# GpSimd head by head, a ring of three for masked scores, and six value-output products made early in a fused attention and feed-forward kernel

## Chip, cores and metric

The kernel runs on one core of a Trainium2 chip. The metric is the device time of one execution in microseconds (us). Engines are called TensorE (PE), VectorE (DVE), ScalarE (ACT), GpSimd (POOL) and SyncE (SP), which issues the DMAs.

## What is computed

```python
# x is (2, 512, 512); 32 heads; ranks 192 (query) and 64 (key/value)
xn = layernorm(x)
q = rmsnorm(xn @ Wq_a, q_a_ln_w) @ Wq_b          # per head 128 + 64 (rotated)
ckv = xn @ Wkv_a
compressed, k_pe = ckv[..., :64], ckv[..., 64:]
kv = rmsnorm(compressed, kv_a_ln_w) @ Wkv_b      # per head 128 key + 128 value
scores = (q_nope . k_nope + rope(q_pe) . rope(k_pe)) * 192 ** -0.5
probs = softmax(where(causal, scores, min))
o = concat_heads(probs @ v) @ Wo
x = x + layernorm(o)
x = x + layernorm(ffn(layernorm(x)))             # silu(gate) * up, tiled weights plus rank-2 terms
```

## The kernel before

The work has four stages. The **first stage** (a loop over `t`, eight token blocks of 128) normalises x, turns it, multiplies by the low-rank weights and turns the results into `ql` and `kt`. The **attention** runs over 16 pairs of heads, `body(p)` on each engine. The **projection** multiplies by the products of value and output weights. The **feed-forward** part ends the kernel.

One pair is 16 units `k` (two batches, two heads, four query blocks of 128; block `i = k % 4` has `128 * (i + 1)` keys). The steps of a unit cross the engines: `scores` on PE (three matmuls into bank `k % 2`), `mask_and_max` on DVE (bank to `ss`), `exponent` on ACT (`ss` to `pr`), `turn_p` on PE, `move_p` on ACT, `output` on PE. At step k PE issues `scores` for unit k+2 ahead of `turn_p` for unit k, and DVE masks unit k+2. Every engine works its list strictly in the order written, and semaphores tie the lists together: `scores(n)` waits until the units up to n-2 are masked, since it writes over their bank.

Once a pair three other things are woven in:

- The weights of the next pair are formed: `absorb_query` on PE at k = 0, then `weights_hi` on ACT (four copies, at k = 1, lines 388 to 391), then `weights_lo` on DVE (four subtractions at k = 2, lines 652 and 653: two take one operand from a PSUM bank, the last two take both operands, `sq` and `w1_hi` or `w2`, from SBUF). Behind them in DVE's list stand `rotate_own` of the second head and the mask of unit 5.
- The rotated queries of both heads of a batch: `query` on PE, `rotate_swapped` and `rotate_own` on DVE, `add_rotated` on GpSimd (line 325), `query_hi` on ACT (line 397), `query_lo` on GpSimd (line 332, `qrot` minus `qt_hi`, both in SBUF). The result `qt_lo` is waited for by `scores` of that head.
- `absorb_output(p)` on PE at k = 8 (line 1087) multiplies a pair's value and output weights (`sv`, loaded by SP); ACT copies the bank to `vs` at k = 9 and SP stores it to DRAM, from where the projection reads it. It is needed by nothing in the attention.

In the last pair (15) there are no next weights. In pair 0 `weights_hi` stands at k = 3 and `weights_lo` at k = 4.

Of the kernel before, what the change touches and what calls it, by code (L numbers as in the profile page):

```python
# [40 lines left out]
XB = 5  # L41
# [3 lines left out]
UNITS = 2 * QB  # L45
PU = BATCH * UNITS
HID, RANK = 1376, 2
# [29 lines left out]
def build(nc, x_d, wa_d, lnw_d, cst_d, kcs_d, sq_d, sv_d, w13_d, bs_d, a13_d, a2_d, w2_d, b2_d, out_d):  # L77
# [34 lines left out]
    ss = att.take("ss", [P, 2, SEQ])  # L112
# [3 lines left out]
    att.at += 32 + 4 * QB * 2 * RKV  # L116
    pt = att.take("pt", [P, 2, 2, QB, SEQ])
    r8 = qswp[0:2 * QB, 0, 0:P]
    negmax = small[:, 0:8]
# [80 lines left out]
    def sems(phase, words):  # L200
# [5 lines left out]
        q_scaled q_doubled qn_made krot_parts kvn_made qk_turned qk_hi_made qk_split""")  # L206
    x_in = [nc.alloc_semaphore(f"x_in{t}") for t in range(TB)]
# [13 lines left out]
    with block:  # L221

        @block.sync
        def _(sp):
# [10 lines left out]
            sp.dma_start(sv[:, :], sv_d[0]).then_inc(a.sv_in, 16)  # L235
# [25 lines left out]
            load_sq(1)  # L261
            load_sq(2)
            send_r(0)
            load_sv(1)
            store_wvo(0)
            for p in range(1, PAIRS - 2):
                send_r(2 * p - 1)
                load_sq(p + 2)
                send_r(2 * p)
                load_sv(p + 1)  # L270
                store_wvo(p)
            send_r(2 * PAIRS - 5)
            send_r(2 * PAIRS - 4)
            load_sv(PAIRS - 1)
            store_wvo(PAIRS - 2)
# [3 lines left out]
            for k in range(PAIRS // 2):  # L279
                if k == 3:  # L280
                    send_r(2 * PAIRS - 2)
                if k == 4:
                    store_wvo(PAIRS - 1)
                if k >= 3:
                    sp.wait_ge(c.wv_split, 2 * (k - 2))
                if k == PAIRS // 2 - 1:
                    send_r(2 * PAIRS - 1)
                    sp.wait_ge(a.wvo_out, 16 * PAIRS)
                sp.dma_start(wv_raw[:, k % 3, :, :], wvo_d[2 * k:2 * k + 2].rearrange("a p n -> p a n"))\
                  .then_inc((c.wv_in0, c.wv_in1, c.wv_in2)[k % 3], 16)  # L290
# [20 lines left out]
        def _(pool):  # L311
# [23 lines left out]
            def body(p, last=False):  # L335
                for b in (1,) if last else (1, 0):
                    gi = 4 * p + (2 if b else 4)
                    pool.wait_ge(a.qt_split, gi)
                    for h in range(2):
                        add_rotated(gi + h, h)  # L340
                    for h in range(2):
                        query_lo(gi + h, b, h, gi + 2)
# [32 lines left out]
        def _(act):  # L375
# [23 lines left out]
            def exponent(U, k, s_first=False, old=None):  # L399

                n = P * (k % QB + 1)
                act.wait_ge(a.s_masked, U + 1)
                if not s_first:
                    act.wait_ge(a.p_turned, U - 3)
                if old is not None:
                    act.wait_ge(a.rinv_made, old)
                nc.scalar.activation(pr[:, k % 4, 0:n], ss[:, k % 2, 0:n], ACT.Exp, bias=negmax[:, k % 8:k % 8 + 1],  # L407
                                     scale=-1.0, accum_out=rsum[:, k:k + 1]).then_inc(a.exp_made, 1)
# [55 lines left out]
            def body(p, first=False, last=False):  # L464
                for k in range(PU):
# [18 lines left out]
                    if k in (2, 4):  # L484
                        h = (k - 2) // 2
                        query_hi(4 * p + 2 + h, 1, h, None if first else PU * (p - 1) + UNITS + QB * (h + 1))
                    if k in (10, 12) and not last:
                        h = (k - 10) // 2
                        query_hi(4 * p + 4 + h, 0, h, PU * p + QB * (h + 1))
                    if k == 9:  # L490
                        act.wait_ge(a.wvo_made, p + 1)
                        if not first:
                            act.wait_ge(a.wvo_out, 16 * p)
# [9 lines left out]
            for t in range(TB + 4):  # L503
                if 0 <= t - 3 < TB:
# [8 lines left out]
                      .then_inc(f.std_rms_made, 1)  # L513
                if 0 <= t - 1 < TB:
# [25 lines left out]
                if t == TB + 2:  # L540
                    exponent(0, 0, True)
# [102 lines left out]
        def _(dve):  # L644
# [26 lines left out]
            def mask_and_max(U, k, first=False):  # L671
# [3 lines left out]
                if not first:  # L675
                    dve.wait_ge(a.exp_made, U - 1)
                nc.vector.tensor_tensor_reduce(out=ss[:, k % 2, 0:n], in0=bank[k % 2][:, 0:n], in1=mask[:, SEQ - n:SEQ],  # L677
# [92 lines left out]
            for t in range(TB + 4):  # L770
# [44 lines left out]
                if t in (TB, TB + 1):  # L815
                    rotate_swapped(t - TB, t - TB, first=True)
                    rotate_own(t - TB, t - TB, first=True)
                if t in (TB + 2, TB + 3):
# [195 lines left out]
        def _(pe):  # L1014
# [68 lines left out]
            def absorb_output(p):  # L1083

                pe.wait_ge(a.sv_in, 16 * (p + 1))
                for h in range(2):
                    last = nc.tensor.matmul(bank[XB][RKV * h:RKV * (h + 1), :], sv[:, h * RKV:(h + 1) * RKV],  # L1087
                                            sv[:, 2 * RKV + h * D:2 * RKV + (h + 1) * D], start=True, stop=True)
# [16 lines left out]
            def body(p, first=False, last=False):  # L1105
                for k in range(PU):
# [5 lines left out]
                    if k == (2 if first else 0) and not last:  # L1112
                        if first:
                            pe.wait_ge(f.qk_split, TB - 1)
                        else:
                            pe.wait_ge(a.wvo_moved, p)
# [7 lines left out]
                    if k == 8:  # L1124
                        if last:
                            pe.wait_ge(a.wvo_moved, p)
                        else:
                            pe.wait_ge(a.wq_split, p + 2)
                        absorb_output(p)
# [18 lines left out]
            for t in range(TB + 4):  # L1148
# [20 lines left out]
                if t == TB:  # L1169
                    pe.wait_ge(f.qk_split, QB)  # L1170
                    for h in range(2):
# [12 lines left out]
                if t == 4:  # L1184
                    absorb_query(0)
                if t in (TB + 2, TB + 3):
# [184 lines left out]
```

## Time and profile before

| what | value |
|---|---|
| median of 3 runs | 632.92 us (631.91 to 633.07) |
| profiled execution | 632.73 us, its span 630.8 us |
| PE busy in the span | 590.5 us (94%) |
| DVE busy | 461.4 us (73%) |
| ACT busy | 400.0 us (63%) |
| GpSimd busy | 198.9 us (32%) |
| length of one pair in the steady part (233.00 to 258.33) | 25.33 us |

Times within the trace are from the span's start. "Idle" in brackets behind an instruction is how long its engine had stood still, and who let it go. An instruction's record on PE, ACT and DVE includes its pipeline, so that neighbouring records overlap a little.

### The profile page before, as it was taken

To read this page: it belongs to the slowest core of one execution; us is meant where nothing else is said; L and a number is where in the kernel's file an instruction comes from. 1 tells how busy PE (TensorE), PEld (TensorE's weight loads), DVE (VectorE), ACT (ScalarE), POOL (GpSimd) and SP (SyncE) were. 2 spreads that over 40 slices of the span, in tenths; PEclk is the share of its full clock that TensorE was granted. 3 is DMA by queue.
4 is the path that set the end of the run, shared out by engine and by line. 5 is a ranking of instruction groups with operands and counts; after the bars stand their busy time and mean duration, and the time that the engine had idled before them with its cause. 6 is when DMAs were issued, how large, how long until landed. Compare 5 with 4: busy or idle time off the path is not lost.

```text
span 630.8 us, 10967 instructions
## 1 busy us (share of the span) xinstructions
PE 590.5 (94%) x3336; PEld 427.7 (68%) x3336; DVE 461.4 (73%) x1235; ACT 400.0 (63%) x1157; POOL 198.9 (32%) x172
## 2 busy tenths in 40 slices
PE   4786999999999999999999999999989999978996
PEld 4675767677677676776776767767658888754564
DVE  5876677677776777777767777777867888878466
ACT  4454677777777677766776777668753545264343
POOL 3134333443344334433353444344000000024630
PEclk9898999999999999999999999999989999999998
DMA  8100212312132122221331213205465000001003
GB/s 316 31 1 16 87 47 89 95 54 71 56 104 78 48 84 76 78 72 52 97 89 48 82 55 101 71 19 153 154 209 226 2 0 2 0 30 50 1 14 121
DMA packets 19561, 46.93 MB, mean 74 GB/s; under 512 B 2608, under 2 KB 3120, under 8 KB 19248
## 3 DMA queue, kind: packets, MB, share of 16 engines
q1 hardware_dynamic: 19504, 46.23, 22.8%
q8 instruction: 28, 0.46, 0.3%
q14 instruction: 29, 0.24, 0.1%
HBM read 39.80 MB, written 6.42 MB: 73 GB/s over the span
## 4 chain that ended last, share of the span: by engine, by line
PE 50%; issue 15%; DVE 15%; POOL 9%; ACT 9%; DMA 1%; POOLq 0%; SPq 0%; DVEq 0%; ACTq 0%
PE bank L1017 11%; PE bank L1019 9%; PE bank L1018 9%; PE bank L1072 7%; PE bank L1060 6%; POOL qrot L325 6%; ACT pr L407 3%; POOL qt_lo L332 3%; PE bank L1087 3%; DVE qswp L664 2%; DVE qrot L669 1%; DVE ss L677 1%; ACT pt L415 1%; DVE dot L865 1%; ACT qt_hi L397 1%
## 5 line engine op out<-in xcount | busy, mean ns | idle before, releaser
L677 DVE CUSTOM_DVE_ANT_0 ss<-bank,cst 128x128 f32<-128x128 f32 (+3 forms) x256 | 124.2, 490 | 95.6 <-PE bank L1019 75.0
L415 ACT ACTIVATE pt<-bank 128x128 f32<-128x128 f32 (+3 forms) x256 | 110.3, 431 | 88.4 <-PE bank L1060 88.3
L325 POOL TENSOR_TENSOR qrot<-qrot,qswp 64x512 f32<-64x512 f32 x64 | 81.9, 1280 | 208.2 <-DVE qrot L669 208.1
L407 ACT ACTIVATE pr<-ss,small 128x128 f32<-128x128 f32 (+3 forms) x256 | 142.4, 556 | 4.2 <-DVE small L677 4.0
L1060 PE MATMUL bank<-ident,pr 128*128 128x128 f32 x640 | 117.1, 281 | 0.6 <-ACT pr L407 0.6
L1017 PE MATMUL bank<-kt_hi,qt_hi 128*128 128x128 f32 (+3 forms) x256 | 101.0, 395 | 7.9 <-DVE small L677 4.5
L1060 PEld LDWEIGHTS bank<-ident,pr 128*128 128x128 f32 x640 | 74.5, 141 | 49.5 <-ACT pr L407 28.8
L332 POOL TENSOR_TENSOR qt_lo<-qrot,qt_hi 128x512 fp32r<-128x512 f32 x64 | 82.0, 1290 | 29.2 <-ACT qt_hi L397 27.9
L1072 PE MATMUL bank<-pt,kvn 128*64 128x256 f32 (+3 forms) x512 | 86.2, 448 | 0.7 <-ACT pt L415 0.7
L1019 PE MATMUL bank<-kt_hi,qt_lo 128*128 128x128 f32 (+3 forms) x256 | 82.9, 324 | 0.0
L1018 PE MATMUL bank<-kt_lo,qt_hi 128*128 128x128 f32 (+3 forms) x256 | 82.7, 323 | 0.0
L1017 PEld LDWEIGHTS bank<-kt_hi,qt_hi 128*128 128x128 f32 x256 | 48.8, 190 | 17.0 <-DVE small L677 9.1
L1017 PE MATMUL bank<-wv,o_s 128*128 128x512 f32 x128 | 52.2, 408 | 2.4 <-DVE wv L703 2.4
L1018 PE MATMUL bank<-wv,o_s 128*128 128x512 f32 x128 | 51.1, 399 | 0.0
L1019 PE MATMUL bank<-wv,o_s 128*128 128x512 f32 x128 | 51.0, 398 | 0.0
L1019 PEld LDWEIGHTS bank<-kt_hi,qt_lo 128*128 128x128 f32 x256 | 48.6, 190 | 2.8
L407 ACT ACTIVATION_READ_ACCUMULATOR pr<-ss,small 128x1 f32 x256 | 49.8, 194 | 0.0
L1018 PEld LDWEIGHTS bank<-kt_lo,qt_hi 128*128 128x128 f32 x256 | 49.3, 193 | 0.1
L1072 PEld LDWEIGHTS bank<-pt,kvn 128*64 128x64 f32 x512 | 29.9, 135 | 27.7 <-ACT pt L415 11.9
L370 POOL TENSOR_TENSOR fs<-gu 128x512 f32<-128x512 f32 (+1 forms) x6 | 8.2, 1366 | 124.5 <-DVE gu L951 124.3
L663 DVE TENSOR_TENSOR qswp<-bank,cst 32x512 f32<-32x512 f32 x64 | 44.5, 695 | 2.0
L664 DVE TENSOR_TENSOR qswp<-bank,cst 32x512 f32<-32x512 f32 x64 | 44.2, 691 | 0.9
(163 smaller groups left out, 1072.5 us busy)
## 6 DMA issues: line engine op xcount, KB each, us to landing
sv<-sv SPq DMA_DIRECT2D x16, 576.0 KB, 5.0
rsb<-rinv_scratch SPq DMA_DIRECT2D x64, 128.0 KB, 2.9
sq<-sq SPq DMA_DIRECT2D x16, 448.0 KB, 3.3
wvo_scratch<-vs SPq DMA_DIRECT2D x16, 256.0 KB, 4.8
wv_raw<-wvo_scratch SPq DMA_DIRECT2D x8, 512.0 KB, 4.8
xa<-x SPq DMA_DIRECT2D x8, 256.0 KB, 5.0
x<-x SPq DMA_DIRECT2D x1, 2048.0 KB, 9.6
out<-yo SPq DMA_DIRECT2D x8, 256.0 KB, 2.0
```

The costliest lines, as they stand in the source:

```text
L325: nc.gpsimd.tensor_tensor(qrot[RKV:P, h, :], qrot[RKV:P, h, :], qswp[RKV:P, h, :], ALU.add)\
L332: nc.gpsimd.tensor_tensor(qt_lo[:, b, h, :], qrot[:, h, :], qt_hi[:, b, h, :].bitcast(F32), ALU.subtract)\
L407: nc.scalar.activation(pr[:, k % 4, 0:n], ss[:, k % 2, 0:n], ACT.Exp, bias=negmax[:, k % 8:k % 8 + 1], scale=-1.0, accum_out=rsum[:, k:k + ...
L415: nc.scalar.activation(pt[:, b, h, 0:i + 1, i * P:(i + 1) * P], bank[2 + k % 2][:, 0:(i + 1) * P].rearrange("p (j q) -> p j q", q=P), ACT. ...
L663: nc.vector.tensor_tensor(qswp[64:96, h, :], G[96:128, :], sin1[96:128, :], ALU.mult)
L664: nc.vector.tensor_tensor(qswp[96:128, h, :], G[64:96, :], sin1[64:96, :], ALU.mult)
L677: nc.vector.tensor_tensor_reduce(out=ss[:, k % 2, 0:n], in0=bank[k % 2][:, 0:n], in1=mask[:, SEQ - n:SEQ], scale=-SCALE, scalar=3.4e38, op ...
L1017: nc.tensor.matmul(out, w_hi, x_hi, start=start, stop=False)
L1018: nc.tensor.matmul(out, w_hi, x_lo, start=False, stop=False)
L1019: return nc.tensor.matmul(out, w_lo, x_hi, start=False, stop=stop)
L1060: last = nc.tensor.transpose(bank[2 + k % 2][:, j * P:(j + 1) * P], pr[:, k % 4, j * P:(j + 1) * P], ident[:, :])
L1072: last = nc.tensor.matmul(bank[4][RKV * h:RKV * (h + 1), j * P:SEQ], kvn[:, QB * b + j, 0:RKV], pt[:, b, h, j, j * P:SEQ], start=(j == 0), ...
```

## The change

Three edits, of which two move instructions.

1. GpSimd works head by head: per batch it now adds head 0, subtracts head 0, adds head 1, subtracts head 1, where it did both adds and then both subtractions. ACT issues `query_hi` of head 0 at k = 1 and 9 (pair 0: 2 and 9) and that of head 1 at 4 and 12; before it was 2, 4, 10 and 12.
2. `ss` has three buffers. The buffer of unit k is `RING[k]`; DVE waits for the exponent two units back only where the ring reuses a buffer after two units, which by `BACK` is at k = 1 and k = 15.
3. Products 0 to 5 of `absorb_output` are issued in the first stage behind iterations 4 to 7 (`EARLY`: number, bank, copies that must have been made), from six loads `sve` that stand behind x and the constants in SP's list, and are copied by ACT to `pr` and `ss` and stored. In the attention pair p makes product p + 6, so that pairs 10 to 15 make none. The first mask and the first exponent wait until the six stores have landed.

```diff
 UNITS = 2 * QB
+RING = (0, 1, 2, 0, 1, 2, 0, 1, 2, 0, 1, 2, 0, 1, 2, 1)
+BACK = [next(d for d in range(1, 17) if RING[k - d] == RING[k]) for k in range(16)]
 PU = BATCH * UNITS
+EARLY = {4: ((0, 7, 0),), 5: ((1, 7, 1),), 6: ((2, 7, 2), (3, 6, 0)), 7: ((4, 7, 3), (5, 6, 4))}
+NE = 6
...
     qswp = att.take("qswp", [P, 2, SEQ])
-    ss = att.take("ss", [P, 2, SEQ])
+    ss = att.take("ss", [P, 3, SEQ])
...
     vs = att.take("vs", [P, D])
-    att.at += 32 + 4 * QB * 2 * RKV
+    att.at += 32
...
     r8 = qswp[0:2 * QB, 0, 0:P]
+    sve = Map(nc, att.at - 4 * 4 * QB * SEQ, att.at).take("sve", [P, NE, SV_COLS])
+    early = [pr[:, j, :] for j in range(4)] + [ss[:, j, :] for j in range(NE - 4)]
...
         q_scaled q_doubled qn_made krot_parts kvn_made qk_turned qk_hi_made qk_split""")
+    sve_in = [nc.alloc_semaphore(f"sve_in{j}") for j in range(NE)]
...
             sp.dma_start(cst[:, :], cst_d).then_inc(f.cst_in, 16)
-            sp.dma_start(sv[:, :], sv_d[0]).then_inc(a.sv_in, 16)
+            for j in range(NE):
+                sp.dma_start(sve[:, j, :], sv_d[j]).then_inc(sve_in[j], 16)
+            sp.dma_start(sv[:, :], sv_d[NE]).then_inc(a.sv_in, 16)
...
-            load_sq(1)
-            load_sq(2)
-            send_r(0)
-            load_sv(1)
-            store_wvo(0)
-            for p in range(1, PAIRS - 2):
-                send_r(2 * p - 1)
-                load_sq(p + 2)
+            for j in range(NE):
+                if j == 2:
+                    load_sq(1)
+                sp.wait_ge(a.wvo_moved, j + 1)
+                sp.dma_start(wvo_d[j], early[j]).then_inc(a.wvo_out, 16)
+            for p in range(PAIRS - 1):
+                if p:
+                    send_r(2 * p - 1)
+                if p + 2 < PAIRS:
+                    load_sq(p + 2)
                 send_r(2 * p)
-                load_sv(p + 1)
-                store_wvo(p)
-            send_r(2 * PAIRS - 5)
-            send_r(2 * PAIRS - 4)
-            load_sv(PAIRS - 1)
-            store_wvo(PAIRS - 2)
+                if p + NE + 1 < PAIRS:
+                    load_sv(p + NE + 1)
+                if p + NE < PAIRS:
+                    store_wvo(p + NE)
...
                     send_r(2 * PAIRS - 2)
-                if k == 4:
-                    store_wvo(PAIRS - 1)
...
                 for b in (1,) if last else (1, 0):
-                    gi = 4 * p + (2 if b else 4)
-                    pool.wait_ge(a.qt_split, gi)
                     for h in range(2):
-                        add_rotated(gi + h, h)
-                    for h in range(2):
-                        query_lo(gi + h, b, h, gi + 2)
+                        gi = 4 * p + (2 if b else 4) + h
+                        pool.wait_ge(a.qt_split, gi)
+                        add_rotated(gi, h)
+                        query_lo(gi, b, h, gi + 1)
...
                     act.wait_ge(a.rinv_made, old)
-                nc.scalar.activation(pr[:, k % 4, 0:n], ss[:, k % 2, 0:n], ACT.Exp, bias=negmax[:, k % 8:k % 8 + 1],
+                nc.scalar.activation(pr[:, k % 4, 0:n], ss[:, RING[k], 0:n], ACT.Exp, bias=negmax[:, k % 8:k % 8 + 1],
...
                         weights_hi(p + 1)
-                    if k in (2, 4):
-                        h = (k - 2) // 2
+                    if k in ((2, 4) if first else (1, 4)):
+                        h = k // 4
                         query_hi(4 * p + 2 + h, 1, h, None if first else PU * (p - 1) + UNITS + QB * (h + 1))
-                    if k in (10, 12) and not last:
-                        h = (k - 10) // 2
+                    if k in (9, 12) and not last:
+                        h = k // 12
                         query_hi(4 * p + 4 + h, 0, h, PU * p + QB * (h + 1))
-                    if k == 9:
-                        act.wait_ge(a.wvo_made, p + 1)
-                        if not first:
-                            act.wait_ge(a.wvo_out, 16 * p)
+                    if k == 9 and p + NE < PAIRS:
+                        act.wait_ge(a.wvo_made, p + NE + 1)
+                        act.wait_ge(a.wvo_out, 16 * (p + NE))
...
                       .then_inc(f.std_rms_made, 1)
+                for j, b, _ in EARLY.get(t - 1, ()):
+                    act.wait_ge(a.wvo_made, j + 1)
+                    nc.scalar.activation(early[j], bank[b][:, :], ACT.Copy).then_inc(a.wvo_moved, 1)
...
                 if t == TB + 2:
+                    act.wait_ge(a.wvo_out, 16 * NE)
...
                 dve.wait_ge(a.s_made, U + 1)
-                if not first:
+                if BACK[k] == 2 and not first:
                     dve.wait_ge(a.exp_made, U - 1)
-                nc.vector.tensor_tensor_reduce(out=ss[:, k % 2, 0:n], in0=bank[k % 2][:, 0:n], in1=mask[:, SEQ - n:SEQ],
+                nc.vector.tensor_tensor_reduce(out=ss[:, RING[k], 0:n], in0=bank[k % 2][:, 0:n], in1=mask[:, SEQ - n:SEQ],
...
                     rotate_own(t - TB, t - TB, first=True)
+                if t == TB + 2:
+                    dve.wait_ge(a.wvo_out, 16 * NE)
...
-            def absorb_output(p):
...
-                pe.wait_ge(a.sv_in, 16 * (p + 1))
+            def absorb_output(j, b=XB, w=sv):
...
+                pe.wait_ge(a.sv_in if j >= NE else sve_in[j], 16 * (j - NE + 1) if j >= NE else 16)
                 for h in range(2):
-                    last = nc.tensor.matmul(bank[XB][RKV * h:RKV * (h + 1), :], sv[:, h * RKV:(h + 1) * RKV],
-                                            sv[:, 2 * RKV + h * D:2 * RKV + (h + 1) * D], start=True, stop=True)
+                    last = nc.tensor.matmul(bank[b][RKV * h:RKV * (h + 1), :], w[:, h * RKV:(h + 1) * RKV],
+                                            w[:, 2 * RKV + h * D:2 * RKV + (h + 1) * D], start=True, stop=True)
...
                         else:
-                            pe.wait_ge(a.wvo_moved, p)
+                            pe.wait_ge(a.wvo_moved, min(p + NE, PAIRS))
...
                         output(2 * p - 1, 1, [2, 3])
-                    if k == 8:
-                        if last:
-                            pe.wait_ge(a.wvo_moved, p)
-                        else:
-                            pe.wait_ge(a.wq_split, p + 2)
-                        absorb_output(p)
+                    if k == 8 and p + NE < PAIRS:
+                        pe.wait_ge(a.wq_split, p + 2)
+                        absorb_output(p + NE)
...
                     pe.wait_ge(f.qk_split, QB)
+                    pe.wait_ge(a.wvo_moved, NE)
...
                     absorb_query(0)
+                for j, b, moved in EARLY.get(t, ()):
+                    if j == 3:
+                        pe.wait_ge(a.wq_split, 1)
+                    if moved:
+                        pe.wait_ge(a.wvo_moved, moved)
+                    absorb_output(j, b, sve[:, j, :])
```

On GpSimd in any pair from 1 to 14 (`qrot` is the rotated query, `qt_lo` its low part), rows of the kernel before:

```order
L325 TENSOR_TENSOR qrot<-qrot,qswp 64x512 x2
L332 TENSOR_TENSOR qt_lo<-qrot,qt_hi 128x512 x2
L325 TENSOR_TENSOR qrot<-qrot,qswp 64x512 x2
L332 TENSOR_TENSOR qt_lo<-qrot,qt_hi 128x512 x2
L325 TENSOR_TENSOR qrot<-qrot,qswp 64x512 x2
```

and of the changed kernel:

```order
L332 TENSOR_TENSOR qrot<-qrot,qswp 64x512
L339 TENSOR_TENSOR qt_lo<-qrot,qt_hi 128x512
L332 TENSOR_TENSOR qrot<-qrot,qswp 64x512
L339 TENSOR_TENSOR qt_lo<-qrot,qt_hi 128x512
L332 TENSOR_TENSOR qrot<-qrot,qswp 64x512
```

The subtraction of the first head has moved ahead of the addition of the second.

On ACT in a pair from 1 to 14, steps k = 1 to 3 (`w_hi` and `w_58` are the next pair's weights), rows of the kernel before:

```order
L407 ACTIVATE pr,small<-ss,small 128x512
L388 ACTIVATE w_hi<-bank 128x2x64
L389 ACTIVATE w_hi<-sq 128x2x64
L390 ACTIVATE w_58<-bank 128x2x64
L391 ACTIVATE w_58<-sq 128x2x64
L415 ACTIVATE pt<-bank 128x3x128
L407 ACTIVATE pr,small<-ss,small 128x128
L397 ACTIVATE qt_hi<-qrot 128x512
```

and of the changed kernel:

```order
L413 ACTIVATE pr,small<-ss,small 128x512
L394 ACTIVATE w_hi<-bank 128x2x64
L395 ACTIVATE w_hi<-sq 128x2x64
L396 ACTIVATE w_58<-bank 128x2x64
L397 ACTIVATE w_58<-sq 128x2x64
L403 ACTIVATE qt_hi<-qrot 128x512
L421 ACTIVATE pt<-bank 128x3x128
```

The copy to `qt_hi` now follows straight behind the four weight copies, two instructions earlier.

On PE at the end of iteration 6 of the first stage (products with `wa`, then the turns of x), rows of the changed kernel, where before the turns of x followed the products at once:

```order
L1029 MATMUL bank<-wa_lo,xt_hi 128x320
L1030 MATMUL bank<-wa_hi,xt_lo 128x320
L1098 MATMUL bank<-sve 64x512 x4
L1163 MATMUL bank<-ident,xn 128x128 x4
L1174 MATMUL bank<-ident,qn 128x128
```

Two early products (four rows of 64x512) stand between them.

## Rows read from the trace of the kernel before

**Rows 1.** Stretches: length, PE, PEld, DVE, ACT, POOL busy, clock share, DMA

```profile
233.00:258.33 25.33, 25.00 (x155) 17.77 (x154) 18.36 (x52) 18.58 (x60) 10.24 (x9) 1.00 0.25 75
```

**Rows 2.** Waits, whole run: us in total, times, longest us

```profile
DVE ss L677 <- ACT pr L407: 19.5, 31, 0.7
...
PEld bank L1017 <- POOL qt_lo L332: 7.0, 15, 2.9
...
PE bank L1017 <- DVE small L677: 4.5, 15, 0.7
```

**Rows 3.** Timeline of PE, a steady pair

```profile
238.70 0.50 PE L1017 MATMUL bank<-kt_hi,qt_hi 128*128 128x512 f32 x1 [0.27 <-DVE small L677]
```

**Rows 4.** Timeline of DVE, the same pair

```profile
236.99 0.29 DVE L652 TENSOR_TENSOR w_lo<-sq,w_hi 128x128 fp32r<-128x128 f32 x1
237.29 0.29 DVE L653 TENSOR_TENSOR w<-sq,w 64x128 fp32r<-64x128 f32 x1
237.61 0.69 DVE L669 TENSOR_TENSOR qrot<-bank,cst 128x512 f32<-128x512 f32 x1
238.22 0.41 DVE L677 CUSTOM_DVE_ANT_0 ss<-bank,cst 128x256 f32<-128x256 f32 x1
...
252.61 0.69 DVE L677 CUSTOM_DVE_ANT_0 ss<-bank,cst 128x512 f32<-128x512 f32 x1 [0.60 <-ACT pr L407]
...
254.87 0.42 DVE L677 CUSTOM_DVE_ANT_0 ss<-bank,cst 128x256 f32<-128x256 f32 x1 [0.66 <-ACT pr L407]
```

**Rows 5.** Timeline of ACT, the same pair

```profile
236.02 0.32 ACT L391 ACTIVATE w<-sq 128x128 fp32r<-128x128 f32 x1
236.22 0.50 ACT L415 ACTIVATE pt<-bank 128x384 f32<-128x384 f32 x1
...
250.88 0.62 ACT L397 ACTIVATE qt_hi<-qrot 128x512 fp32r<-128x512 f32 x1
```

**Rows 6.** Timeline of GpSimd, the same pair

```profile
251.64 1.30 POOL L332 TENSOR_TENSOR qt_lo<-qrot,qt_hi 128x512 fp32r<-128x512 f32 x1 [0.72 <-ACT qt_hi L397]
```

**Rows 7.** Timelines of POOL, DVE and PE in pair 0

```profile
58.14 1.26 POOL L332 TENSOR_TENSOR qt_lo<-qrot,qt_hi 128x512 fp32r<-128x512 f32 x1
...
59.37 1.31 POOL L332 TENSOR_TENSOR qt_lo<-qrot,qt_hi 128x512 fp32r<-128x512 f32 x1
...
58.50 1.06 DVE L652 TENSOR_TENSOR w_lo<-sq,w_hi 128x128 fp32r<-128x128 f32 x1
59.57 1.25 DVE L653 TENSOR_TENSOR w<-sq,w 64x128 fp32r<-64x128 f32 x1
...
60.88 0.80 PE L1017 MATMUL bank<-ql_hi,w_hi 128*128 128x512 f32 x1 [3.75 <-DVE w L653]
```

**Rows 8.** Timelines of POOL and DVE in the feed-forward part

```profile
565.17 1.40 POOL L370 TENSOR_TENSOR fs<-fs,gu 128x512 f32<-128x512 f32 x1 [1.24 <-DVE gu L951]
...
565.01 0.41 DVE L881 TENSOR_TENSOR w_lo<-w,w_hi 128x256 fp32r<-128x256 f32 x1
565.34 1.78 DVE L865 CUSTOM_DVE_ANT_0 dot<-xn,a 128x512 f32<-128x512 f32 x1
```

**Rows 9.** Chain that ended last: one product in a pair

```profile
244.46 1.01 PE bank L1087 x4
```

**Rows 10.** Stretches of the first stage and pair 0, columns as rows 1

```profile
23.14:27.28 4.14, 1.51 (x11) 1.01 (x10) 4.00 (x15) 2.19 (x10) 0.38 (x2) 0.91 0.14 17
27.28:33.38 6.10, 6.10 (x24) 6.06 (x25) 4.83 (x21) 2.26 (x9) 1.09 (x4) 0.50 0.18 69
33.38:39.28 5.90, 5.90 (x38) 5.48 (x37) 4.85 (x16) 1.84 (x8) 0.55 (x2) 1.00 0.00 0
...
60.68:64.09 3.41, 3.21 (x10) 2.62 (x10) 0.84 (x3) 0.24 (x1) 0.00 (x0) 0.50 0.49 134
```

**Rows 11.** DMA issues: count, KB each, us to landing

```profile
wvo_scratch<-vs SPq DMA_DIRECT2D x16, 256.0 KB, 4.8
```

**Rows 12.** Timeline of DVE, the first mask

```profile
45.90 0.28 DVE L677 CUSTOM_DVE_ANT_0 ss<-bank,cst 128x128 f32<-128x128 f32 x1
```

## The prediction, made before the result was known

> **What bounds the kernel now.** I first cut the steady part into pairs with the view of stretches. One pair lasts 25.33 us, with PE busy for 25.00 of them at full clock, while DVE and ACT are busy for some 18 and GpSimd for 10 [rows 1]. So PE sets the pace and the others follow it. What shortens a pair is PE work taken out, or one of PE's few waits; what lengthens it is any delay that reaches PE, since PE has nothing in hand to make it up with. The view of waits names those waits: in each of pairs 1 to 14 PE stops about 0.3 us for a mask (line 677), and its weight load stops for `qt_lo`, 7.0 us in all, of which 2.9 in the first stage, so 4.1/14 = 0.29 us a pair. DVE waits for the exponent 31 times, 19.5 us in all [rows 2].
>
> The timeline shows which mask that is: the 512-key scores at 238.70, let go by DVE [rows 3]. On DVE the mask ahead of it is the 256-key one at 238.22, and in front of that stand `rotate_own` and the four subtractions of `weights_lo`, the last two at 236.99 and 237.29 [rows 4]. They start as soon as ACT has made the four weight copies, the last at 236.02 to 236.34 [rows 5]. This stretch of DVE, from ACT's copies to the mask, is the one place of a pair where DVE and not PE ends the wait. Whatever delays it delays PE, one for one.
>
> **Ring of three.** The two stops of DVE for the exponent in a pair are at the 512-key mask of 252.61 (k = 15) and the 256-key mask of 254.87 (k = 1) [rows 4], twice 15 and one more. Those are exactly the two units at which the new ring still reuses a buffer after two units and keeps the wait. PE stands for neither of them. I cost this edit at nothing, and a gain on DVE there (at most 0.6 + 0.7 us) would be hidden behind PE. If that cover were gone, the most it could give is those 19.5 us.
>
> **Head by head.** `qt_lo` of head 0 no longer waits for the addition of head 1, so the stop of 0.29 us [rows 2] goes; next in line is the mask two units back, already made. I take 0.2 us of it, 14 times: **-2.8 us** (bounds 0 and -4.1). In pair 0 the two subtractions of GpSimd, which held DVE's `weights_lo` up to 60.82 and with it PE for 3.75 us [rows 7], are spread: the second addition (near 57.6 to 58.9) holds the first subtraction of DVE to about 59.05, the second follows at once, and PE starts near 59.4 in place of 60.88: **-1.5 us** (if the slow clock behind that stop, 3.41 us at 0.50 [rows 10], also goes, another 1.7 us).
>
> **What the earlier copy to `qt_hi` collides with.** This is the large term. At k = 1 ACT now copies head 0 straight behind the weight copies. The next ACT record there starts 0.20 us after the last weight copy does, at 236.22 [rows 5]; the copy takes 0.62 us, so it ends at 236.84. GpSimd follows such a copy by 0.14 us (250.88 + 0.62 = 251.50, and 251.64) [rows 5, 6]. So its subtraction of 1.30 us starts at about 236.98, and DVE's first subtraction with both operands in SBUF at 236.99, the second at 237.29 [rows 4]. Before the change GpSimd did nothing then.
>
> Pair 0 shows what such a meeting costs. GpSimd worked from 58.14 to 59.40 and from 59.37 to 60.68; the two DVE subtractions took 1.06 and 1.25 us in place of 0.29, ending at 59.56 and 60.82 [rows 7]. The first ended 1.42 us after GpSimd's start, the second 1.45 us after the second one's. The feed-forward part shows the order of arrival: GpSimd came at 565.17 into a running DVE subtraction, was held 0.1 us and then ran, and the DVE operation that came next took 1.78 us [rows 8]. So even when DVE's first operation is in front, GpSimd gets in between the two and the second one waits.
>
> The two ends for a pair: if the second ends at 236.98 + 1.45 = 238.43 against 237.58, the delay is 0.85 us; if the first ends at 236.98 + 1.42 = 238.40 and the second 0.30 later, it is 1.12 us. A row for DVE slipping both in first does not exist in two of the meetings, but the starts lie 0.01 us apart, so the lower bound is 0. I take 1.0 us, between the two measured ends. Behind it queue `rotate_own`, the mask of 238.22, then PE's scores of 238.70, so PE gets all of it: 14 pairs (1 to 14; pair 15 has no weights to form) x 1.0 = **+14.0 us** (11.9 to 15.7; 0 if it does not happen). At k = 9 the same move meets no DVE operation with two SBUF operands.
>
> The Trainium skill says of this (SBUF — State Buffer, Who interferes with whom) that a VectorE instruction with two SBUF inputs and a GpSimd instruction that reads SBUF exclude each other for a whole instruction, and that the order of issue decides who is held. By that rule alone the sum would be either the one above or, if VectorE is first both times, the one of the second case below. It speaks against this change, and the rows of pair 0 agree with it.
>
> **Six early products.** One product is 1.01 us of PE [rows 9]. Pairs 10 to 15 lose theirs. Nothing else is late at k = 8: what follows needs exponents and masks that in the trace are done before, and they move with PE. Five whole ones and, since DVE splits projection weights in pair 15, 0.8 for the last: **-5.9 us** (bounds 0 and -6.1). In the first stage they cost something. The first two fall behind iterations 4 and 5, where PE is busy 1.51 of 4.14 us while DVE is busy 4.00 [rows 10]; free. The other four stand behind iterations 6 and 7, in a stretch in which PE is busy without a break from 27.28 to 39.28, so they add 4.0 us. But from 27.28 to 33.38 PE ran at 0.50 of its clock (the level of 1.2 GHz) after standing for most of the stretch before [rows 10]; the early products fill part of that idle time. If PE stays at its 2.4 GHz level, that stretch shortens by half, 3.05 us. I take 4.0 - 3.0 = **+1.0 us** (up to +4.0). The stores take 4.8 us to land [rows 11]; the last copy has to be made by about 37, so they are down some 4 us ahead of the first mask at 45.90 [rows 12]. Loads behind those of x cost nothing; without that cover each costs what its transfer is late.
>
> **Sum.** -2.8 - 1.5 + 14.0 - 5.9 + 1.0 = +4.8 us. Against the profiled execution's 632.73 us, which stands 0.2 under the median shown, that is **637.5 us**.
>
> **Rivals.**
> - *The collision doesn't bite.* DVE gets both subtractions in ahead of GpSimd, or GpSimd starts some 0.3 us later than I read. Then the sum is -9.2 us, 623.5 us. For it: the starts are 0.01 us apart and GpSimd's records are rough. Against it: rows 7 and 8. The collision decides as long as it costs over 9.2/14 = 0.66 us a pair.
> - *Collision, but the clock pays.* At the lower end of 0.85 (+11.9) and with the slow stretch of pair 0 gone too (-1.7), the sum is 4.8 - 2.1 - 1.7 = +1.0: about no change, 633.7 us.
> - *The four early products run at the low level.* PE falls to 0.50 as before and the first stage takes all 4.0 us: 4.8 + 3.0 = +7.8, 640.5 us. Idle time before them is only partly filled, which speaks for it.
>
> **How the numbers follow.** A measurement of this kernel can tell from no change about 0.2%, 1.3 us. Forecast and the low-level case are slower: 0.54 and 0.14. The case at 633.7 has 0.10, spread on both sides of the bound. The one without collision has 0.22. That makes faster 0.22, same 0.10, slower 0.68. The forecast's own range is 634.5 to 641; to leave no more than 2 in 10 out, the range has to reach to the case without collision, so 623 to 641.5.
>
> **What the profile after will show.** If I am right: `w_lo<-sq` or `w<-sq` on DVE with means over 0.9 us in place of 0.29, PE's wait for the mask at 1.2 to 1.4 us a pair, pairs of about 26.1 us up to 9 and 25.1 from 10 to 14, no wait for `qt_lo`, DVE still waiting for the exponent twice a pair. If those two DVE groups stay at 0.29 us, the prediction is wrong, and pairs are 25.1 and 24.1 us long. The first stage is right if the product of iteration 8 ends near 40.3, and PE is not at 0.50 between 27 and 33.

## The result: 0.9% slower, and the profile after

The changed kernel takes 638.1 us (median of 7 runs, 635.1 to 639.2), the kernel before on the same chip 631.9 (7 runs, 631.5 to 633.1): a ratio of 1.0086 with a 95% interval of 1.0067 to 1.0106. The prediction was 637.5 us. The profiled execution took 638.9 us with a span of 637.1; it stands 0.8 us above the median and 6.2 above the profiled execution of before, for which the prediction's sum gave +4.8. The medians are 6.2 apart as well.

The top of the page of after, with busy time, share and instruction count of each engine:

```profile
span 637.1 us, 10771 instructions
PE 586.8 (92%) x3336; PEld 427.1 (67%) x3336; DVE 472.7 (74%) x1235; ACT 402.2 (63%) x1157; POOL 201.0 (32%) x172
```

One pair of after, in the view of stretches (columns as in [rows 1]):

```profile
220.88:246.88 26.00, 24.73 (x155) 17.73 (x155) 19.37 (x53) 18.75 (x60) 10.40 (x9) 1.00 0.24 72
```

Against [rows 1] the pair is 0.67 us longer and PE is busy for 0.27 us less of it, so PE now stands for 1.27 us of a pair in place of 0.33. Where it stands, the timeline of PE says (start, duration, instruction, and in brackets the idle time and what ended it):

```profile
220.88 0.50 PE L1028 MATMUL bank<-kt_hi,qt_hi 128*128 128x512 f32 x1 [1.25 <-DVE small L686]
...
246.88 0.50 PE L1028 MATMUL bank<-kt_hi,qt_hi 128*128 128x512 f32 x1 [1.26 <-DVE small L686]
```

These are the 512-key scores of [rows 3], where the stop was 0.27 us. DVE's timeline over the same place shows what came late, to be read beside [rows 4]:

```profile
243.86 0.29 DVE L662 TENSOR_TENSOR w<-bank,w 64x128 fp32r<-64x128 f32 x1
244.17 0.29 DVE L661 TENSOR_TENSOR w_lo<-sq,w_hi 128x128 fp32r<-128x128 f32 x1
244.47 1.28 DVE L662 TENSOR_TENSOR w<-sq,w 64x128 fp32r<-64x128 f32 x1
245.79 0.69 DVE L678 TENSOR_TENSOR qrot<-bank,cst 128x512 f32<-128x512 f32 x1
246.40 0.41 DVE L686 CUSTOM_DVE_ANT_0 ss<-bank,cst 128x256 f32<-128x256 f32 x1
```

and the timelines of ACT and of GpSimd show why:

```profile
243.21 0.32 ACT L397 ACTIVATE w<-sq 128x128 fp32r<-128x128 f32 x1
243.41 0.63 ACT L403 ACTIVATE qt_hi<-qrot 128x512 fp32r<-128x512 f32 x1
...
244.18 1.42 POOL L339 TENSOR_TENSOR qt_lo<-qrot,qt_hi 128x512 fp32r<-128x512 f32 x1 [2.90 <-ACT qt_hi L403]
```

ACT's copy starts 0.20 us behind the last weight copy and ends at 244.04, and GpSimd follows 0.14 us later. By then DVE's first subtraction with both operands in SBUF (244.17) has just started, 0.01 us ahead (0.01 to 0.02 in all pairs from 1 to 14). It is not held. GpSimd's operation is recorded 0.14 us longer than its usual 1.28, and DVE's second subtraction takes 1.28 us in place of 0.29 and ends 1.57 us behind GpSimd's start. Mask and scores follow it. All pairs look like this one, as the groups of DVE's instructions by shape show (total, mean ns, idle time before):

```profile
L662 DVE TENSOR_TENSOR w<-sq,w 64x128 fp32r<-64x128 f32 x16 | 18.5, 1155 | 0.2
L661 DVE TENSOR_TENSOR w_lo<-sq,w_hi 128x128 fp32r<-128x128 f32 x16 | 5.0, 310 | 0.2
L662 DVE TENSOR_TENSOR w<-bank,w 64x128 fp32r<-64x128 f32 x16 | 4.7, 294 | 0.2
```

The view of waits, where [rows 2] had PE's stops for `qt_lo` and 31 stops of DVE for the exponent:

```profile
POOL qt_lo L339 <- ACT qt_hi L403: 85.7, 54, 2.9
PEld bank L1028 <- DVE small L686: 22.6, 15, 1.6
PE bank L1028 <- DVE small L686: 18.0, 15, 1.3
DVE ss L686 <- ACT pr L413: 9.6, 15, 0.6
PEld bank L1028 <- POOL qt_lo L339: 2.9, 1, 2.9
```

In pair 0 PE's stop for the weights is down from the 3.75 us of [rows 7]:

```profile
62.79 0.80 PE L1028 MATMUL bank<-ql_hi,w_hi 128*128 128x512 f32 x1 [2.29 <-DVE w L662]
```

The first stage, in stretches that answer to [rows 10]: the first begins with the products of iteration 6 and ends at 33.38 as there, the second ends where the products of iteration 8 end, and the last two are the stretches at the lower of the two clock levels (0.50, 1.2 GHz).

```profile
27.49:33.38 5.89, 5.89 (x36) 4.32 (x37) 5.26 (x22) 3.36 (x13) 1.09 (x4) 1.00 0.58 192
33.38:40.83 7.45, 7.45 (x42) 5.40 (x41) 5.06 (x15) 3.14 (x10) 0.54 (x2) 1.00 0.23 87
48.44:55.29 6.85, 5.60 (x16) 3.81 (x15) 2.14 (x8) 3.76 (x12) 1.33 (x2) 0.51 0.01 2
62.02:68.85 6.83, 6.06 (x20) 5.18 (x21) 2.93 (x10) 2.58 (x7) 1.54 (x2) 0.50 0.21 67
```

With the early products PE holds 1.00 from 27 to 41 us, where it was at 0.50 up to 33.38 before; but two later stretches at 0.50 are now twice as long (before: 47.0 to 50.4 and 60.7 to 64.1). Together they come to 13.7 us in both kernels.

**Where the 6.2 us are.** PE's first transpose of sums (a matmul of `small`) stands at k = 8, half-way through pair 0. It comes 3.2 us later than before (71.28 against 68.06), and so does the end of the pair. From there to the last transpose of sums (at 466.76, before 460.13) it is 395.48 us against 392.07, 3.4 more. The projection and the feed-forward part give the rest, -0.4.

### The profile page after: what moved, and what is told of

Its sections match the earlier page's. It is cut to its first block and busy times, and to the rows that moved or that the text cites. A ratio compares the mean times of both kernels' runs of the same rounds, so it can differ in the third digit from the quotient of the medians.

```text
span 637.1 us, 10771 instructions
## 1 busy us (share of the span) xinstructions
PE 586.8 (92%) x3336; PEld 427.1 (67%) x3336; DVE 472.7 (74%) x1235; ACT 402.2 (63%) x1157; POOL 201.0 (32%) x172
## 5 line engine op out<-in xcount | busy, mean ns | idle before, releaser
L339 POOL TENSOR_TENSOR qt_lo<-qrot,qt_hi 128x512 fp32r<-128x512 f32 x64 | 83.9, 1311 | 111.1 <-ACT qt_hi L403 85.7
```

Source lines behind the costliest of these rows:

```text
L339: nc.gpsimd.tensor_tensor(qt_lo[:, b, h, :], qrot[:, h, :], qt_hi[:, b, h, :].bitcast(F32), ALU.subtract)\
```

## Experiments

Each ratio below is against the kernel before, run on the same chip. Numbers 1 to 4 and 9 to 11 ran on one chip, 5 to 8 on a second and 12 on a third, and the kernel before had medians from 631.5 to 632.7 us there: where two numbers of different chips are compared, the ratios go before the times. Pair lengths are PE's, between the same two instructions one pair apart.

**1. The subtractions of `weights_lo` in the other order** (6 runs). The two with both operands in SBUF go first, the two with a bank operand last.

```diff
-                for cols, src in ((slice(0, RKV), pv), (slice(RKV, P), rv)):
+                for cols, src in ((slice(RKV, P), rv), (slice(0, RKV), pv)):
```

> The changed kernel with the four subtractions of the weights on VectorE in another order: the two with both operands in SBUF first, the two with one operand in a bank last. If GpSimd's read of SBUF holds VectorE's last subtraction, the collision is gone: the last subtraction of each kind takes 0.29 us in pairs 1 to 14, the TensorE wait for the mask falls from 1.26 to 0.3 us, a pair is 25.0 us in place of 26.0, and the time 638.1 - 14 x 1.0 = 624 us. If it is the earlier copy on ScalarE that delays the path, and the port has no part in it, nothing changes: 638 us.

626.5 us (624.2 to 628.9), 0.991 [0.989, 0.993]. The pair is 25.03 us. The timelines of DVE and of GpSimd:

```profile
238.53 0.29 DVE L661 TENSOR_TENSOR w_lo<-sq,w_hi 128x128 fp32r<-128x128 f32 x1 [0.78 <-ACT w L397]
238.84 0.29 DVE L662 TENSOR_TENSOR w<-sq,w 64x128 fp32r<-64x128 f32 x1
239.14 0.29 DVE L661 TENSOR_TENSOR w_lo<-bank,w_hi 128x128 fp32r<-128x128 f32 x1
239.44 0.29 DVE L662 TENSOR_TENSOR w<-bank,w 64x128 fp32r<-64x128 f32 x1
239.77 0.69 DVE L678 TENSOR_TENSOR qrot<-bank,cst 128x512 f32<-128x512 f32 x1
...
239.16 1.29 POOL L339 TENSOR_TENSOR qt_lo<-qrot,qt_hi 128x512 fp32r<-128x512 f32 x1 [2.91 <-ACT qt_hi L403]
```

GpSimd starts at the same distance behind ACT, and now meets two subtractions and `rotate_own` that read a bank. None of them is held. The same number of the same instructions is 0.97 us shorter in a pair. So it is not more work that cost the time, but that two instructions of two SBUF operands met a GpSimd one.

**2. The first copy to `qt_hi` one unit later** (6 runs), as in the kernel before; all else is as changed.

```diff
-                    if k in ((2, 4) if first else (1, 4)):
-                        h = k // 4
+                    if k in (2, 4):
+                        h = (k - 2) // 2
```

> The changed kernel with the copy of head 0 at k = 2 again, as before the change; GpSimd still works head by head. If the collision is the cause, GpSimd starts 0.7 us later, behind the last subtraction: 624 us, pairs of 25.0 us. If it is GpSimd's new order by itself that costs time, the time stays at 638 us.

624.6 us (622.3 to 626.9), 0.988 [0.985, 0.990]; pair 25.03. Taking the GpSimd operation away from the subtractions and taking the subtractions away from it give the same pair.

**3. The copy ahead of the weight copies** (10 runs): at k = 1 ACT makes `query_hi` first, `weights_hi` behind it.

```diff
+                    if k in ((2, 4) if first else (1, 4)):
+                        h = k // 4
+                        query_hi(...)
                     if k == (3 if first else 1) and not last:
                         weights_hi(p + 1)
-                    if k in ((2, 4) if first else (1, 4)):
-                        h = k // 4
-                        query_hi(...)
```

> The changed kernel with the copy of head 0 ahead of the weight copies of k = 1 in place of behind them. If the collision is the cause: GpSimd's subtraction ends before VectorE reaches the operands in SBUF, all four subtractions take 0.29 us, but they start 0.5 us later, so the TensorE wait is 0.27 + 0.5 = 0.8 us in place of 1.26: 638.1 - 14 x 0.5 = 631 us. If the early copy costs time by itself, this is no faster than 638 us.

630.9 us (627.7 to 633.2), 0.997 [0.996, 0.999]; pair 25.55. The subtractions are back at 0.29 us, but they all start later, and PE still stands for the mask:

```profile
215.27 0.50 PE L1028 MATMUL bank<-kt_hi,qt_hi 128*128 128x512 f32 x1 [0.79 <-DVE small L686]
```

**4. Two buffers for masked scores** (6 runs).

```diff
-RING = (0, 1, 2, 0, 1, 2, 0, 1, 2, 0, 1, 2, 0, 1, 2, 1)
+RING = (0, 1) * 8
```

> The changed kernel with two buffers of masked scores in turn, as before. If the third buffer does nothing (its two waits are the ones that were there): 638 us, within 1.3 us, with two waits of VectorE for the exponent a pair. If it hides something on the way to TensorE, it is slower by up to 0.6 us a pair, 646 us.

637.7 us (635.0 to 642.3), 1.010 [1.006, 1.013], and the pair is 26.00. Even DVE's wait for the exponent is as before: 10.1 us, 16 times, against 9.6, 15 times, with three buffers. So the drop from 31 waits to 15 came with the new timing of the units and not with the third buffer. Numbers 5 and 12 say the same from the other side: 16 waits with edit 1 and two buffers, 30 with three buffers and without edit 1.

**5. Head by head alone** (4 runs): the kernel before, with GpSimd and ACT as in the change, two buffers, no early product.

> The kernel before with edit 1 alone (head by head, copies at k = 1, 4, 9 and 12), no ring, no early products. By the measured pairs (26.00 against 25.33 us) and the shorter stop in pair 0: 631.9 + 14 x 0.67 - 1.5 = 640 us. If the loss of the whole change lies in the first stage, this is no slower than 632 us.

638.8 us (637.8 to 639.4), 1.011 [1.009, 1.013]; pair 26.00, and the second SBUF subtraction has a median of 1.28 us. The whole loss is in this one part of the change, which alone loses a little more than all three together (1.0086).

**6. The change without its early products** (4 runs): all sixteen products stand in the pairs.

```diff
-EARLY = {4: ((0, 7, 0),), 5: ((1, 7, 1),), 6: ((2, 7, 2), (3, 6, 0)), 7: ((4, 7, 3), (5, 6, 4))}
-NE = 6
+EARLY = {}
+NE = 0
...
```

Their loads, stores and waits go with them.

> The changed kernel without the early products: each pair makes its own, as before; head by head and the ring stay. Pairs 10 to 15 get their 5.9 us back, the first stage and pair 0 lose the 3.2 us that the early products and the clock cost there: 638.1 + 5.9 - 3.2 - 1.5 = 639 us. If early products were worth their full 5.9 us, it would be 644 us; if worth nothing, 638 us.

639.1 us (638.6 to 639.4), 1.012 [1.010, 1.013]; pair 26.00. By the times the six early products bring 1.0 us, by the ratios 1.8, and the two intervals overlap; the terms of the sum gave 4.9.

**7. `weights_lo` one unit later** (6 runs), behind the mask that PE was waiting for.

```diff
-                    if k == (4 if first else 2) and not last:
+                    if k == (4 if first else 3) and not last:
                         weights_lo(p + 1)
```

> The changed kernel with VectorE's four weight subtractions one step later (k = 3, behind the mask of unit 5), the copy of head 0 still at k = 1, so that the collision stays but has cover. If TensorE waits only because the mask stands behind the subtractions, the last subtraction still takes about 1.0 us or more, and yet the TensorE wait of 1.26 us is gone, with the 0.27 us that was there before the change: 638.1 - 14 x 1.4 = 618 us. If the collision costs TensorE in another way, it stays above 630 us.

629.5 us (628.0 to 630.9), 0.996 [0.994, 0.998]: 11.5 us off the 618 expected. PE's wait for the mask is gone, and another has come (views of waits, of DVE's, GpSimd's and PE's timelines):

```profile
PEld bank L1028 <- DVE w L662: 18.9, 15, 2.7
PE bank L1028 <- DVE w L662: 12.3, 15, 2.3
...
238.22 1.03 DVE L661 TENSOR_TENSOR w_lo<-sq,w_hi 128x128 fp32r<-128x128 f32 x1
239.26 1.35 DVE L662 TENSOR_TENSOR w<-sq,w 64x128 fp32r<-64x128 f32 x1
240.64 0.56 DVE L686 CUSTOM_DVE_ANT_0 ss<-bank,cst 128x384 f32<-128x384 f32 x1
...
237.82 1.28 POOL L339 TENSOR_TENSOR qt_lo<-qrot,qt_hi 128x512 fp32r<-128x512 f32 x1 [2.91 <-ACT qt_hi L403]
239.18 1.28 POOL L332 TENSOR_TENSOR qrot<-qrot,qswp 64x512 f32<-64x512 f32 x1
...
240.67 0.50 PE L1028 MATMUL bank<-ql_hi,w_hi 128*128 128x512 f32 x1 [0.71 <-DVE w L662]
```

With `weights_lo` later, `rotate_own` of head 1 stands ahead of it, so GpSimd has its next addition ready and works from 237.82 to 240.46 with hardly a gap. Each of DVE's two subtractions falls under one of its operations and is held, 0.74 and 1.06 us. I had looked at who waits for the mask and not at what GpSimd does in the new place. The pair is 25.46 us.

**8. Both moves together** (4 runs): `weights_lo` at k = 3 and the copy at k = 2.

> As wlo_k3, with the copy of head 0 at k = 2. If the collision under cover is free, the same 618 us, within 1.3 us; if it still reaches TensorE, by the query that waits for the weights, one of the two is clearly faster.

615.4 us (615.0 to 619.6), 0.976 [0.972, 0.979], the fastest of all. The pair in the view of stretches, and the two engines around `weights_lo`:

```profile
215.45:239.93 24.48, 24.48 (x157) 17.74 (x156) 18.45 (x53) 18.62 (x59) 10.40 (x8) 1.00 0.25 77
```

```profile
232.78 0.29 DVE L661 TENSOR_TENSOR w_lo<-sq,w_hi 128x128 fp32r<-128x128 f32 x1
233.09 0.29 DVE L662 TENSOR_TENSOR w<-sq,w 64x128 fp32r<-64x128 f32 x1
...
233.14 1.39 POOL L339 TENSOR_TENSOR qt_lo<-qrot,qt_hi 128x512 fp32r<-128x512 f32 x1 [3.67 <-ACT qt_hi L403]
```

PE doesn't stand once in a pair of 24.48 us. Against number 2, which differs by the place of `weights_lo` alone, that is 0.55 us less, though PE's stop there was recorded at 0.27: a stop costs more than PE's idle time shows. PEld's wait for the same mask is nearer (median 0.58 us in number 2, 1.10 in number 3 and 1.56 in the change, and their pairs are 0.55, 1.07 and 1.52 us longer than 24.48). Here GpSimd comes 0.05 us behind the start of the second subtraction, and there is no third for it to hold. Against the change the pair is 1.52 us shorter; 14 of them are 21.3 of the 22.7 us between the medians.

**9 to 12. What each part is worth once PE no longer stands** (4 runs each). The first is number 8 without early products:

> The fastest kernel so far (weight subtractions at k = 3, copy of head 0 at k = 2, 615.4 us) without the early products. Up to the start of the attention's steady part, at equal time of slow TensorE clock, kernels with early products were 4.5 to 5.0 us later than those without, against 5.9 us that pairs 10 to 15 give back. So the early products are worth about 1 us: 616.4 us. If they were worth their full 5.9 us: 621.3 us.

620.0 us (618.4 to 621.2), 0.982 [0.979, 0.985]; pair 24.48. That is 3.6 us off the 616.4 expected. The second is number 8 with two early products, those of iterations 4 and 5 (`load_sq(1)` also stands one store earlier):

```diff
+EARLY = {4: ((0, 7, 0),), 5: ((1, 7, 1),)}
+NE = 2
...
```

> The same with two early products, those behind iterations 4 and 5 of the first stage, where TensorE waits anyway; pairs 14 and 15 make none. If the first two are free and the other four are paid for in the first stage: 4 x 1.01 us given up in the pairs, about the same gained in the first stage, so 615 us, within 1.5 us. If all six are free: 619.4 us.

620.6 us (618.7 to 621.4), 0.983 [0.980, 0.985], nothing gained over none and 5.6 us off the 615 expected. Its profiled execution has a stretch of 3.4 us at 0.50 in pair 15 that the one of number 9 has not. The third is the kernel before with the one line of number 7:

> The kernel before the change with one edit: the weight subtractions on VectorE at k = 3 in place of 2. The TensorE wait of 0.27 us for the mask (0.4 us of lost issue) goes; GpSimd's second addition and first subtraction then meet the last two weight subtractions, under cover until the query that waits for them. Expected 631.9 - 14 x 0.4 = 626 us. If the collision comes through, as in wlo_k3 of the changed kernel (0.7 us a pair), it is 630 us or more.

619.7 us (617.6 to 621.1), 0.981 [0.978, 0.984]; pair 24.48. That is 6 us faster than expected. DVE's `rotate_own` of head 1 now stands ahead of `weights_lo`, so GpSimd's addition of head 1 runs before the subtractions of `weights_lo`, and its subtraction of head 0 starts only in the last of them (first DVE, then GpSimd):

```profile
231.79 0.29 DVE L652 TENSOR_TENSOR w_lo<-sq,w_hi 128x128 fp32r<-128x128 f32 x1
232.10 0.29 DVE L653 TENSOR_TENSOR w<-sq,w 64x128 fp32r<-64x128 f32 x1
...
230.67 1.27 POOL L325 TENSOR_TENSOR qrot<-qrot,qswp 64x512 f32<-64x512 f32 x1 [2.15 <-DVE qrot L669]
232.15 1.40 POOL L332 TENSOR_TENSOR qt_lo<-qrot,qt_hi 128x512 fp32r<-128x512 f32 x1 [0.22 <-ACT qt_hi L397]
```

and so the wait of PE for `qt_lo` is gone as well. A pair is 0.85 us shorter: 0.55 of it is the price of the mask's stop (number 8 against number 2), and 0.30 that of `qt_lo` (number 2 against the kernel before). What the view of waits still shows of it is the first stage's alone:

```profile
PEld bank L1017 <- POOL qt_lo L332: 2.9, 1, 2.9
```

The last is number 8 with GpSimd and ACT in the order of before (both additions, then both subtractions):

> The fastest kernel so far (615.4 us: weight subtractions at k = 3, copy of head 0 at k = 2, ring, six early products) with GpSimd's old order and the copies at k = 2, 4, 10 and 12, so without edit 1. If head by head is worth nothing once the subtractions stand at k = 3, pairs stay at 24.48 us, and only the stop in pair 0 is 1.5 us longer: 617 us. If head by head is what makes the move pay, pairs are 24.8 us or more: 620 us or more.

618.6 us (617.9 to 618.9), 0.979 [0.976, 0.981]; pair 24.48. PE's stop in pair 0 is back:

```profile
64.45 0.80 PE L1029 MATMUL bank<-ql_hi,w_hi 128*128 128x512 f32 x1 [3.76 <-DVE w L663]
```

In the pairs head by head is worth nothing once `weights_lo` has moved. Its 1.5 us in pair 0 are real (2.30 in number 8); the medians differ by 3.3 us (2.1 by the ratios), but up to about 70 us the profiled execution of this kernel spent 10.2 us more at the low clock than that of number 8, so how they divide stays open.

**The first stage in all runs.** For each profiled execution, the start of the first transpose of sums (in pair 0 at k = 8, behind the pair's stop for the weights; "the mark" below), and the time at 0.50 up to about 70 us, from the view of stretches cut where the granted clock changes:

| kernel | early products | the mark, us | at 0.50, us |
|---|---|---|---|
| before | 0 | 68.06 | 13.65 |
| after | 6 | 71.28 | 13.66 |
| 1 | 6 | 72.04 | 17.07 |
| 2 | 6 | 69.23 | 10.24 |
| 3 | 6 | 68.45 | 6.82 |
| 4 | 6 | 72.03 | 13.65 |
| 5 | 0 | 63.55 | 6.83 |
| 6 | 0 | 65.60 | 10.25 |
| 7 | 6 | 68.06 | 6.83 |
| 8 | 6 | 68.57 | 6.83 |
| 9 | 0 | 65.32 | 10.24 |
| 10 | 2 | 64.99 | 6.83 |
| 11 | 0 | 67.58 | 13.65 |
| 12 | 6 | 72.60 | 17.07 |

Three things are to be seen.

- At equal time at the low clock, and with the same stop of 2.3 us in pair 0, six early products bring the mark later than none: at 6.83 us by 4.5 to 5.0 (numbers 3, 7 and 8 against 5), at 10.24 by 3.6 to 3.9 (number 2 against 6 and 9); two of them at 6.83 by 1.4 (number 10 against 5). Part of this lies ahead of the first early product: the turn of the fourth block of x begins anywhere from 15.6 to 17.0 us. Counted from that turn, six early products cost 4.1 to 4.4 us in all five comparisons, close to four at 1.01 us, and two of them 0.8.
- The time at the low clock is anything from 6.8 to 17.1 us among kernels whose first stage is the same but for the order of four subtractions (numbers 1 to 4, 7 and 8). From 6.82 to 13.66 us at the low clock the mark moves by 2.8 us (number 3 and the change, with the same stop in pair 0).
- The low stretches change places with the early products. Between 26 and 34 us none of the eight executions with six early products has any; of the five without, the kernel before has 6.8 us, numbers 6, 9 and 11 have 3.4 and number 5 none. The next low stretch, which begins between 42 and 50 us, lasts 6.8 or 10.2 us in seven of the eight, and 3.4 in all five without. So what the early products gave back at the first place was mostly taken at the second. These are single executions, and why it is so isn't shown.

## Why the prediction was right, step by step

- **The collision** (predicted +14.0 us, 1.0 a pair). Right in place, mechanism and size: ACT's copy, the 0.14 us to GpSimd, the first subtraction ahead by 0.01 us, the second one held, the wait for the mask at 1.26 us (0.99 more). The order of [rows 8] was the one that came. (Where the prediction says that VectorE first both times would be "the second case below", it means the first rival, 623.5 us.) Shown by numbers 1, 2 and 5: it goes if either party is moved, and head by head alone makes all of it. The Trainium skill (SBUF — State Buffer, Who interferes with whom) says that such an instruction and GpSimd's exclude each other for a whole instruction, and the trace agrees, with 1.28 us in place of 0.29. Number 1 adds that the ones with a bank operand were not held.
- **Head by head** (-2.8, 0.2 a pair). The pair grew by 0.67 us with 0.99 of wait added, so this gave back 0.32 a pair, 4.5 us in 14. The term was sized too small: the whole 0.29 of [rows 2] went, and not 0.2 of it. Numbers 1 and 2 show it without the collision, with pairs of 25.03 us in place of 25.33.
- **Pair 0** (-1.5). 3.75 to 2.29 us, -1.46. The low clock behind that stop, which might have gone too, got longer.
- **Ring of three** (0). Right, shown by number 4. What was said of DVE's waits was wrong: they fell from two to one a pair, and the one at the 512-key mask of k = 15 went, though the ring keeps it; with two buffers again there are as few waits.
- **Six early products in the pairs** (-5.9). A pair behind the ninth lasts 24.91 us in place of 26.00. From the mark on the pairs took 3.4 us more, and 14 x 0.67 = 9.4, less 3.4, leaves 6.0. Number 6, the change without early products, takes 401.36 us there in place of 395.48: 5.9, as predicted.
- **First stage** (+1.0). This is the mis-sized term. Up to iteration 8 it went nearly as said: the stretch from 27 to 33 us ran at 1.00, and the product of iteration 8 ended at 40.83, +1.55. The first mask came 1.55 later too (47.45 against 45.90). But the 3.0 us counted for the clock there did not last: the low stretches at two later places doubled, and from the first mask to the mark it is 23.83 us in place of 22.16, although the stop of pair 0 is 1.46 shorter. The mark came 3.2 us later, where first stage and pair 0 together were to give -0.5. With pair 0's -1.5 taken out, the first stage cost 4.7 us at equal time at the low clock: the bound of +4.0 given for no help of the clock, and a little over. The rival "the four early products run at the low level" named about the right price (+4.0) with the wrong place. The step of this term that failed is to take the clock's gain in one stretch of one profile as a gain of the whole: number 5, with no early product, had no low stretch between 26 and 34 us either, and what the early products gained there was mostly lost behind 45 us.
- **The sum.** +4.8 was predicted and +6.2 found. Head by head (-1.7), the first stage and pair 0 (+3.7) and the part behind the pairs (-0.4) are the difference; the rest is rounding. Two misses of opposite sign hide part of each other, and that the median (638.1) lies only 0.6 us from the forecast of 637.5 is luck as well: the kernel before came out 0.8 us below the execution from which the sum was counted. The direction and the large term are not luck.

What stays open is the net worth of the early products: 1.0 us by number 6 against the change (639.1 and 638.1; by the ratios 1.8), 4.7 by number 9 against number 8 (620.0 and 615.4; by the ratios 4.1). The pairs' 5.9 less the 4.1 to 4.4 of the first stage at equal time at the low clock gives 1.5 to 1.8. Number 10, with two products that were to be free, is no faster than number 9 with none, though its mark comes 0.3 us earlier. The low clock moves single executions by more than these differences, and the runs don't settle it.

Four expectations missed. In number 7 the step "the mask wait goes and nothing takes its place" failed: the place to which `weights_lo` moved was one in which GpSimd had two operations in a row. In number 11 the same blind spot was in the other direction: the same line put the addition and the subtraction of GpSimd on either side of the subtractions, and freed `qt_lo` as well; the mask's stop was also worth 0.55 us and not 0.4. Numbers 9 and 10 missed by 3.6 and 5.6 us, and both rested on the worth of the early products, which stays open.

## What to carry to other kernels

When a GpSimd operation is made to start earlier, list the VectorE instructions with both operands in SBUF at its new time, and price each meeting at up to a whole GpSimd operation (here 1.28 us long, of which 1.0 reached the pair, 14 times); if one is found, move either of the two or let the VectorE instructions with a PSUM operand take the place beside it. Check the new place of whatever is moved in the same way: one line of order was worth 12 us in the kernel before, and the same line in the changed kernel only 8.6 until GpSimd was moved too. Price a stop of TensorE by the wait of its weight load as well as by its idle time (0.58 against 0.27 us here, and 0.55 gained when it went). Work that fills idle time of TensorE early in a kernel is to be judged at the end of that part and over several runs, since the granted clock can give back at one place and take at the next.

## What the runs showed of the hardware that was not expected

- Of two back-to-back VectorE instructions with two SBUF operands, a GpSimd operation that comes 0.01 to 0.02 us behind the start of the first gets in between, every time: the first one keeps its 0.29 us, the second takes 1.27 to 1.28 (14 of 14 in pairs 1 to 14). GpSimd's own record is 0.14 us longer when it came 0.01 us behind (1.42), and 0.11 longer when it came 0.05 behind (1.39), less than the 0.28 and 0.24 us that were left of the VectorE instruction.
- When GpSimd has two operations in a row, both of VectorE's are held (1.03 and 1.35 us in number 7, in all 14 pairs), so VectorE gets in once between GpSimd's, and GpSimd once between VectorE's.
- GpSimd's recorded start doesn't always tell who was first: in the kernel before, an operation recorded from 581.30 us on took 3.32 us, while a VectorE subtraction that started at 581.74, 0.44 us behind it, was over after 1.74 us.
- A stop of TensorE for a mask, recorded as 0.27, 0.79 and 1.26 us of idle time, made the pair 0.55, 1.07 and 1.52 us longer (numbers 2 and 3 and the change, against number 8).
- The stretches in which the granted clock fell to 0.50 differed in number, place and length (3.4 to 10.2 us) between executions of kernels with the same first stage.
